# A message-passing layer's edge stage in blocks of 24 full tiles, its gathers issued pair by pair after landings

## The reference

```python
x, src, dst, edge_attr_64        # (12500, 128) f32, (400000,), (400000,) sorted, (400000, 64)
h = jnp.maximum(_layernorm(x, axis=-1), 0.0)
m_in = jnp.concatenate([h[src], edge_attr], axis=1)
messages = jax.nn.relu(m_in @ msg_w1 + msg_b1) @ msg_w2 + msg_b2
aggregated = jax.ops.segment_sum(messages, dst, num_segments=12500)
u = jax.nn.relu(jnp.concatenate([h, aggregated], axis=1) @ upd_w1 + upd_b1)
out = x + u @ upd_w2 + upd_b2
```

## Time and profile before

| what | value |
|---|---|
| median of 3 runs | 4913.87 us (4913.0 to 4914.27) |
| the profiled execution's own time | 4917.07 us |
| its span, first to last instruction | 4915.3 us |
| busy: POOL, PE, PEld, DVE, ACT | 79%, 71%, 65%, 46%, 12% |
| TensorE clock granted, mean | 0.608 of full speed |
| memory traffic | 68 GB/s over the span |

### The profile page before, as it was taken

The page is one execution under the profiler, slowest core; times in us unless marked ns, Lnnn a source line. Parts: engine busy times, 40 slices in busy tenths (PEclk is TensorE's granted clock), DMA queues, the critical chain, the costliest instruction groups (busy, mean ns, idle before and its releaser), DMA issues.

```text
span 4915.3 us, 59369 instructions
## 1 busy us (share of the span) xinstructions
PE 3511.1 (71%) x16139; PEld 3183.0 (65%) x16139; DVE 2248.7 (46%) x3651; ACT 595.7 (12%) x887; POOL 3881.7 (79%) x3208
## 2 busy tenths in 40 slices
PE   5677777777677767766777677767776677767766
PEld 3666666666666666666666666666666666666666
DVE  5455555555444444444444444444444444444444
ACT  5111111111100000001010001000100010001002
POOL 7777777777778787877777777777777777777774
PEclk8666666666655555556555655655565655565566
DMA  7322222222222222222222222222222222222223
GB/s 174 73 67 64 69 66 67 68 66 67 64 64 64 65 65 64 64 64 64 64 66 64 64 64 65 64 64 64 65 65 64 64 64 66 64 64 64 65 64 87
DMA packets 398534, 336.04 MB, mean 68 GB/s; under 512 B 287275, under 2 KB 304299, under 8 KB 397263
## 3 DMA queue, kind: packets, MB, share of 16 engines
q0 software_dynamic: 256000, 208.52, 18.0%
q1 hardware_dynamic: 141810, 126.99, 10.5%
q10 hardware_dynamic: 706, 0.33, 0.0%
HBM read 319.26 MB, written 12.81 MB: 68 GB/s over the span
## 4 chain that ended last, share of the span: by engine, by line
POOL 72%; issue 23%; PE 2%; SPq 1%; DMA 1%; POOLq 0%; DVE 0%; another core or an unknown queue 0%; ACT 0%; ACTq 0%; DVEq 0%
POOL rows L380 72%; SPq L281 1%; PE pre L542 0%; POOLq L374 0%; PE seg L403 0%; DMA rows<-table,index 0%; PE pre L407 0%; PE pre L395 0%; POOLq L378 0%; DMA table<-space 0%; PE seg L467 0%; DMA b_upd_col<-in_b_upd 0%; DVE space L716 0%; PE iota_ps L542 0%
## 5 line engine op out<-in xcount | busy, mean ns | idle before, releaser
L380 POOL DMA_INDIRECT rows<-table,index x3125 | 3789.7, 1213 | 953.9 <-issue 953.0
L467 PE MATMUL seg<-space,hidden 125*128 125x128 f32 x6400 | 1517.1, 420 | 1030.1 <-ACT hidden L613 697.5
L467 PEld LDWEIGHTS seg<-space,hidden 125*128 125x128 f32 x6400 | 1353.0, 316 | 1166.2 <-issue 640.8
L785 DVE TENSOR_TENSOR hidden<-pre,rows 125x640 f32<-125x640 f32 x625 | 514.9, 824 | 1826.4 <-DMA rows<-table,index 1614.0
L433 PE MATMUL pre<-w_attr_sb,attr_space 64*125 64x128 f32 x6250 | 1304.0, 384 | 15.1 <-issue 15.1
L433 PEld LDWEIGHTS pre<-w_attr_sb,attr_space 64*125 64x125 f32 x6250 | 1173.1, 284 | 116.1 <-issue 103.7
L613 ACT ACTIVATE hidden<-hidden 125x640 f32<-125x640 f32 x640 | 471.5, 737 | 4247.4 <-DVE hidden L785 3476.0
L834 DVE TENSOR_REDUCE part_space<-space 125x128 f32<-125x640 f32 x640 | 790.6, 1235 | 0.0
L826 DVE TENSOR_TENSOR space<-iota_ps,dst_rel 125x640 f32<-125x640 f32 x640 | 526.0, 822 | 118.3 <-DVE part_space L834 71.1
L476 PE MATMUL seg<-part_space,w_msg_t_sb 128*128 128x128 f32 x1280 | 393.4, 407 | 224.8 <-DVE part_space L834 208.4
L476 PEld LDWEIGHTS seg<-part_space,w_msg_t_sb 128*128 128x128 f32 x1280 | 319.8, 306 | 258.7 <-issue 258.5
(11 more groups left out here) (65 smaller groups left out, 503.9 us busy)
## 6 DMA issues: line engine op xcount, KB each, us to landing
attr_space<-in_attr SPq DMA_DIRECT2D x640, 156.2 KB
rows<-table,index POOLq DMA_INDIRECT x3125
index<-in_src SPq DMA_DIRECT2D x625, 2.4 KB
table<-space SPq DMA_DIRECT2D x25, 224.0 KB
out<-x_all SPq DMA_DIRECT2D x4, 1120.0 KB
x_all<-in_x SPq DMA_DIRECT2D x2, 1120.0 KB
x_all<-in_x SPq DMA_DIRECT2D x1, 2240.0 KB
attr_space<-in_dst_rows SPq DMA_DIRECT2D x2, 781.2 KB
```

The lines of the kernel that those rows point to most:

```text
L380: pool.indirect_dma_start(rows[0:EDGES, k, t, :], None, table, bass.IndirectOffsetOnAxis(index[:, k, t:t + 1], 0))\
L467: last = pe.matmul(seg[:, 0, 0:WINDOW], hidden[0:EDGES, hidden_slot(k), t * D:(t + 1) * D], mask[:, k % 2, t, :], start=(t == 0), stop=(t ...
L785: dve.tensor_tensor(hidden[0:EDGES, k, :], pre[0:EDGES, k % 2, 0:TILES * D], rows[0:EDGES, k].rearrange("p t d -> p (t d)"), ALU.add).then ...
```

## The change

It rewrites the edge stage, how gathers are released, and the final stage. The parts, with the names that the diff has:

- **Tiles of 128 edges** (`EDGES`), 3125 in all; a pair is 8 tiles (`PAIR`), a block is 3 pairs (`TILES_B` = 24 tiles). There are 130 blocks and a last one of 5 tiles. Early blocks, gathered from `x`, are 3 (72 gathers instead of 75 for 15 chunks).
- **POOL** issues a pair's gathers after the pair before has landed, and from block 8 on waits for the one-hot products of block b - 4 (`LEAD`).
- **Buffers**: 8 slots of a block, four of them over `x_all`, whose rows are loaded again at the end; `hidden` is written in place over the gathered rows. Attributes of one block come in one load of 128 partitions by 1536 columns, two buffers.
- **PE**: two tiles of attributes stand above each other on 128 partitions, against a weight of 128 x 256 with two diagonal blocks: 12 matmuls of 256 columns a block. The one-hot is 80 columns wide (`WINDOW`), and each pair has its own base; update sums are 2 matmuls of 240 columns a block.
- **DVE**: masks, mask sums and the copy once a block, `sum_rows` once a pair, three additions to `update` a block.
- **Final stage**: nodes are grouped by number, and 24 of the 25 groups are finished from block 112 on, when no later edge can reach them (`FINISH`), by ACT loading and storing them; one is left for the end (`REST`).
- The node stage is the same work; POOL still waits for all table stores before the first gather of the table.

```diff
-EDGES = 125
+EDGES = 128
 UNROLL = 5
-TILES = 5
-CHUNK = TILES * EDGES
-WINDOW = 128
+PAIR = 8
+PAIRS = 3
+TILES_B = PAIRS * PAIR
+SLOTS = 8
+AHEAD = 5
+LEAD = 4
+WINDOW = 80
 WIDE = 256
-EARLY = 15
+EARLY = 3
...
+            def gather(source, j, tiles):
+                for t in tiles:
+                    pool.indirect_dma_start(slot_rows(j)[:, t, :], None, source, bass.IndirectOffsetOnAxis(index[0:EDGES, j, t:t + 1], 0))\
+                        .then_inc(gathered[j][t // PAIR], 16)
+
+            def gather_block(i, j):
+                b = block_of(i, j)
+
+                if isinstance(i, int) and i == 0:
+                    pool.wait_ge(index_next_loaded, 16)
+                else:
+                    pool.wait_ge(index_loaded[j], i * 16)
+                if not isinstance(b, int) or b >= SLOTS:
+                    pool.wait_ge(hidden_summed, b - LEAD + 1)
+                for q in range(pairs_of(b)):
+                    before_i, before_j, before_q = (i, j, q - 1) if q else (*behind(i, j, 1), PAIRS - 1)
+
+                    pool.wait_ge(gathered[before_j][before_q], before_i * (16 * PAIR) + 16 * PAIR)
+                    pool.sem_inc(pool_turns, 1)
+                    gather(table, j, range(q * PAIR, q * PAIR + tiles_of(b, q)))
...
+            def attr_product(i, j, q, two, stop):
+                start = q * COLUMNS + two * EDGES
+                return pe.matmul(columns(j, q, PAIR)[:, two * 2 * D:(two + 1) * 2 * D], attrs[:, j % 2, start:start + EDGES],
+                                 w_attr_sb[:, :], start=True, stop=stop)
...
+                    last = pe.matmul(seg[:, j % 2, q * WINDOW:(q + 1) * WINDOW], slot_rows(j)[:, q * PAIR + t, :],
+                                     mask[:, j % 2, q, t, :], start=(t == 0), stop=(t == tiles - 1))
...
+                pe.matmul(spare[:, 0:width], w_both[:, :], part[:, j % 2, 0:width], start=True, stop=False)
+                pe.matmul(spare[:, 0:width], bias_both[0:EDGES, :], mask_sum[:, j % 2, 0:width], start=False, stop=True)\
+                    .then_inc(seg_ready, 1)
...
+                for q in range(pairs_of(b)):
+                    s = b * PAIRS + q
...
+                    sum_rows(i, j, q)
...
+                    if q == 1:
+                        sum_masks(*behind(i, j, 1))
+                    if q == 2:
+                        copy_sums(*behind(i, j, 1))
+                        accumulate(*behind(i, j, 2))
```

More of the change, by code:

```diff
@@ new lines, in load_block @@
+            def load_block(i, j):
+                b = block_of(i, j)
+                nxt = ahead(i, j, AHEAD)
+                if exists(*nxt) and not (isinstance(b, int) and b + AHEAD < SLOTS):
+                    need(sp, summed, b * PAIRS + (PAIRS - (SLOTS - AHEAD) * PAIRS))
+                    load_index(*nxt)
+                load_attr(i, j)
+            sp.wait_ge(update_ready, after(GROUPS - 1))
+            for j in range(SLOTS):
+                load_block(0, j)
+            with sp.Fori(1, ROUNDS) as i:
+                for j in range(SLOTS):
+                    load_block(i, j)
@@ L384, in _ @@
+            with pool.Fori(1, ROUNDS) as i:
+                for j in range(SLOTS):
+                    gather_block(i, j)
+            for i in range(ROUNDS, -(-(LAST + 1) // SLOTS)):
+                for j in rounds_of(i):
+                    gather_block(i, j)
         @block.tensor
@@ new lines, in update_sums @@
+            def update_sums(i, j):
+                if not exists(i, j):
+                    return
+                b = block_of(i, j)
+                width = pairs_of(b) * WINDOW
+                pe.wait_ge(part_copied, b + 1)
+                pe.wait_ge(mask_sums_made, b + 1)
+                need(pe, accumulated, b * PAIRS)
+                finished = sum(1 for at in FINISH.values() if isinstance(b, int) and at < b + (2 if b < LAST - 2 else 3))
+                need(pe, o_made, finished)
+                pe.matmul(spare[:, 0:width], w_both[:, :], part[:, j % 2, 0:width], start=True, stop=False)
+                pe.matmul(spare[:, 0:width], bias_both[0:EDGES, :], mask_sum[:, j % 2, 0:width], start=False, stop=True)\
+                    .then_inc(seg_ready, 1)
@@ L897, in edge_steps @@
                 if not wide:
[L898 to L901 removed]
+                    finish_groups(i, j)
             def edge_loops(wide):
[L904 to L906 removed]
@@ new lines, in edge_loops @@
+                one = divmod(LAST - 1, SLOTS)
+                two = divmod(LAST, SLOTS)
+                make_masks(*one)
+                for q in range(PAIRS):
+                    if q < PAIRS - 1:
+                        sum_rows(*one, q)
+                    if q == 0:
+                        sum_masks(*behind(*one, 1))
+                        copy_sums(*behind(*one, 1))
+                        accumulate(*behind(*one, 2))
+                    if q == 1:
+                        finish_groups(*one)
@@ new lines, in edge_loops @@
+                make_masks(*two)
+                sum_masks(*one)
+                sum_rows(*one, PAIRS - 1)
+                for q in range(PAIRS_LAST):
+                    sum_rows(*two, q)
+                accumulate(*behind(*one, 1))
+                copy_sums(*one)
+                sum_masks(*two)
+                copy_sums(*two)
+                accumulate(*one)
+                accumulate(*two)
+                dve.wait_ge(accumulated, LAST * PAIRS + PAIRS_LAST)
+                for g in REST:
+                    finish_group(g)
```

968 lines of the change are left out of this document (579 added, 389 removed).

## The result

The kernel after takes 4807.98 us (median of 4 runs, 4803.36 to 4809.7), the kernel before beside it 4914.07 (4913.0 to 4914.63). The ratio is 0.978, 95% interval 0.977 to 0.980: 2.2% faster, where 2.6% slower was forecast. The profiled execution has a span of 4808.0 us.

The account below looks back on a forecast made before the run. POOL, issuing gathers back to back, was taken as the bound: start 126 + gathers 3978 + landing waits 917 + tail 16 = 5037 us of span, forecast as 5040, 2.6% slower; range 4380 to 5760.

Parts of the forecast that it names:

- The frame: Whole kernel: time = start of the table's gathers + gathers x (work + gap) + landing waits + tail, with POOL as bound.
- Price of one gather: POOL's work on one 128-row gather: 1.00 us instead of 1.213, gap of 0.30 unchanged; 3053 x 1.303 = 3978 us.
- Landing wait: POOL waits before every pair for the pair before: 382 times 2.4 us net, 917 us, nothing covers it.
- Start: First gather of the table, set by the table's last store: 126 us, bounded between 0 and 8 us more, taken as 0.
- break-even of 0.956: Price of one gather in us at which the forecast's sum equals 4904 us, 0.2% under the kernel before.
- LEAD zero: POOL's wait for products of block b - 4 never binds in mid-run: zero, at most 30 us once at block 8.
- PE hidden: Edge stage: PE's 25 us a block is hidden under POOL's 38.5, so the PE work saved is worth nothing.
- Tail: From the start of the last gather to the end: 16 us instead of 48.6.
- A price that stays: Rival: a gather still costs 1.213 or 1.242 us; 5692 us, up to 5780; chance 0.24.
- waits of 1.8: Rival: landing waits cost 1.8 us each, 229 us less, 4810 us with the forecast's price; chance 0.05.
- second rival: Gather price falls further, below 0.9 us, as POOL writes less padding; faster, 4428 us at 0.80; chance 0.27.
- the forecast's own case: Price of 0.90 to 1.12 us and waits of 2.2 to 2.75 us: 4660 to 5540 us; chance 0.41.

Follow-up runs that it names:

- e8: Kernel after with 17 lone gathers from `x` of 8 to 128 rows put ahead, each waited for, to measure price by rows; 4882.15 us, one run.
- e3: Kernel after with landing waits also between the nine pairs gathered early from `x`; 4783.28 us, ratio 0.971.
- e2: Kernel after with `LEAD` 8 instead of 4; 4813.32 us, ratio 0.978.
- e18: Kernel after with early pairs' landing waits, no landing waits between table pairs, and an unwaited 1-column POOL write after each table gather; 3960.36 us, ratio 0.806.
- e1: Kernel after without the 382 waits for landings, nothing else changed; 4877.17 us, ratio 0.990.
- e4: Kernel before with tiles of 128 edges instead of 125, nothing else changed; 5655.72 us, ratio 1.150.
- the control above: Unplanned comparison of the early stage most follow-up kernels share, against no kernel: DVE's last table part at 137.1 to 144.5 us on three chips, 90.2 to 92.4 on three.
- e14: Kernel after with early pairs' landing waits, and for the table one 8-column POOL write, waited for, after each 8 gathers instead of landing waits; 4248.44 us, ratio 0.864.
- e13: Kernel after with early pairs' landing waits, and a POOL drain after each table gather instead of landing waits; 10670.34 us, ratio 2.170.

## Why the prediction was wrong

- **The frame held.** POOL bounds the kernel after; the changes of start, gathers, waits and tail add up to the measured change of the span within 4 us, and neither PE nor one-hot products stand in the mid-run chain.
- **Price of one gather: the step that failed, by 5%.** "I give the padding one sixth of the price" took 1.00 us; 0.946 was measured, 3053 x 0.054 = 165 us. The mechanism held as far as the runs can tell: with 128 rows the 1160 bytes beside the rows shrink to 64 (205.00 MB over 3125 gathers of the table and of `x`), and the gather is cheaper. It was mis-sized: 0.27 us went, 22% of the price and not a sixth. The line of e8 gives it as (25 - 8) x 0.0145 = 0.25. The fixed part, which the text named as the argument against a large fall, is most of the price: 0.84 of 0.946. For its sake the estimate of 0.39 us, if all of POOL's work went by rows per engine, is out as well.
- **Landing wait: the second term that was mis-sized, by 12%.** 2.11 us net against 2.4, 382 x 0.29 = 111 us. The estimate built on the 3.36 us of the last 125-row gather's landing; here the gathers before a pause mostly land in 2.5 us:

```profile
4101.06 2.51 DMA x_all<-table,index
```

That row is from the chain of waits.
- **Start: a term missing.** "Bound between 0 and 8 us more" was 45. The text priced SP's queue and left out that gathers at a faster pace can disturb the engines beside them. e3 ties 27 us of it to unbroken early gathers. In the groups on time the start was 127.6 to 129.6, with eight pauses added, and there the table's stores, which the text has as what sets it, no longer did.
- **The sign.** With the forecast's own other terms, the price alone turns it: 5040 - 165 = 4875, faster by 0.8%. The wait alone doesn't: 5040 - 111 = 4929. Beside the late start both errors are needed. With the measured price and start but waits of 2.4 the sum is 1061 + 45 + 3053 x 1.249 = 4919, even; with the measured wait and start but the price of 1.00 it is 5040 - 111 + 45 = 4974, slower. Together, -165 and -111 against +45, they give 4809, and 4808 was measured. The break-even of 0.956 stood in the text and the measured 0.946 lies just beyond it: the forecast leaned to "slower" on a row chosen between 0.61 and 1.24.
- **LEAD zero:** right (e2), at this pace. **PE hidden:** right where signals are on time; in e18 PE is busy 2457 us of 3961 and has 0% of the chain. **Tail:** 18.5 against 16. **Packets well below 80:** right.
- **The rivals.** A price that stays is out, and so is one below 0.9 (0.946), and waits of 1.8 (2.11). The sign of the second rival came true inside the forecast's own case, of which the text had put about a third under before.
- **A rival that was missing:** that the waits aren't pure cost. On the chip of e1 to e4 taking them away made the kernel 1.3% slower; where signals stayed on time, the kernel without them (e18) stands 17% below e3 in ratio, 0.806 to 0.971; of the 823 us between their medians 14 are the start, and the rest is 2.12 us for each of the 382 waits. That compares two chips, which is open to the doubt of the control above.

**Left open.** Why signals and PE's instructions come late under unbroken 128-row gathers; what differs between the groups, chip or occasion; whether e18 would keep its gain on a chip of the other kind; and whether the short waits on "remote" in the node stage of the kernel before (30 us in all on ACT and DVE, each below 3 us, the last part of the table at 120.0 us) are the same thing in small. An unpaused kernel without writes was not run on a chip whose early stage was on time, and e18 was not run on one where it was late; these two runs would settle what the write does.

## What to carry to other kernels

Price an indirect gather by the rows of its fullest transfer engine and not by its rows: going from 125 to 128 took 22% off each, and one odd tile of 127 takes 2.7 times POOL's work for one of 128. When a sum's sign rests on a price between far bounds, give the break-even first and see how few per cent of error turn it. And when variants are compared across chips, let each carry a stage that the edit can't touch, and look at that stage by its own end, not by what waits for it: here it took away a conclusion that several runs seemed to support.

## What the runs showed of the hardware

- A gather's time on POOL: some 0.84 us + 0.0145 us for each row of the fullest engine, within 0.04 us for 15 gathers of 8 to 128 rows; 127 rows 2.57 us (e8). Bytes beside the rows: 64 + 64 x (rows of the fullest engine - rows / 16), in all 17 gathers of e8. In back-to-back gathers 0.30 us lie between two, and a write of up to 8 columns (0.11 to 0.13 us) fits inside.
- A pause for a landing costs 2.1 us net; a write with a wait after 8 gathers 0.7 net (e14: 1.0 from the end of a gather to the next, instead of 0.30); a drain 2.2 us each time (e13).
- Unbroken 128-row gathers every 1.25 us can delay other engines' signals by 10 to 38 us and spread PE's matmuls to one every 1.4 us (e1). With the 125-row gathers every 1.517 us of the kernel before no wait on "remote" is longer than 3.0 us. It appeared in three of the six groups, and wherever it did, also in the stage that all variants share: that ended at 137 to 145 us in place of 90 to 92.
